# Attention over 16 heads: four engines' loops written out, SyncE's loads put behind its stores, DVE's scaling behind the last split

## What is computed

```python
h = _layernorm(x) * (1 + ca) + sa
Q = (h @ Wq + bq).reshape(B, S, Hn, Dh)         # B=1, S=4096, Hn=16, Dh=16; K and V alike
logits = jnp.einsum('bqhd,bkhd->bhqk', Q, K) * scale
logits = jnp.where(causal, logits, -jnp.inf)
attn = jax.nn.softmax(logits, axis=-1)
gate = jnp.tanh(g @ g_w2 + g_b2)[..., 0]
out = jnp.einsum('bhqk,bkhd->bqhd', attn * gate[:, None, None, :], V).reshape(B, S, E)
x = x + ga * (out @ Wo + bo)
```

## Time and profile before

| | us |
|---|---|
| median of 3 runs | 2980.59 |
| lowest and highest run | 2969.75, 2982.99 |
| profiled execution: span from first to last instruction | 2973.9 |
| PE busy | 2635.1 (89%) |
| DVE busy | 2263.6 (76%) |
| ACT busy | 1646.1 (55%) |
| POOL busy | 214.1 (7%) |

### The profile page before, as it was taken

How to read it: one execution, slowest core, us unless ns; L and a number is a source line. 1 busy time by engine, 2 the same in 40 slices (tenths; PEclk the granted TensorE clock), 3 DMA queues, 4 the chain that set the end, 5 groups by cost and what they waited for, 6 DMA issues and landing times. The chain is left out here.

```text
span 2973.9 us, 94419 instructions
## 1 busy us (share of the span) xinstructions
PE 2635.1 (89%) x36424; PEld 1624.7 (55%) x36424; DVE 2263.6 (76%) x4398; ACT 1646.1 (55%) x2421; POOL 214.1 (7%) x228
## 2 busy tenths in 40 slices
PE   6889999899989998999999978999997999218996
PEld 3332566666656665656557623555554666216774
DVE  3459898789979987999889933655555999685877
ACT  2320777677767776777677765111114777215663
POOL 1237000000000000000000020000000000000000
PEclk8985999999999999999999989999998999659998
DMA  4243011101110111011110001000000333413442
GB/s 141 95 96 72 3 27 28 25 7 28 27 28 4 27 27 28 10 21 27 28 28 5 6 4 53 29 14 28 14 0 8 96 99 103 124 29 100 119 122 64
DMA packets 158662, 133.50 MB, mean 45 GB/s; under 512 B 103097, under 2 KB 135996, under 8 KB 153276
## 3 DMA queue, kind: packets, MB, share of 16 engines
q1 hardware_dynamic: 152571, 124.08, 17.6%
q10 hardware_dynamic: 4224, 4.19, 0.4%
q0 software_dynamic: 1536, 0.40, 0.1%
HBM read 79.98 MB, written 46.66 MB: 43 GB/s over the span
## 5 line engine op out<-in xcount | busy, mean ns | idle before, releaser
L712 DVE TENSOR_REDUCE attn_pm<-attn_MS 128x1 f32<-128x512 f32 (+3 forms) x2304 | 1334.6, 640 | 171.0 <-PE attn_MS L756 144.2
L698 ACT ACTIVATE attn_PT<-attn_ES 128x1024 f32<-128x1024 f32 (+5 forms) x1152 | 1040.0, 951 | 370.8 <-PE attn_ES L791 366.5
L806 PE MATMUL attn_OP<-attn_PT,attn_VH 128*17 128x512 f32 (+3 forms) x4608 | 648.8, 562 | 0.2
L756 PE MATMUL attn_MS<-head_KX,head_QX 96*32 96x512 bf16 (+11 forms) x3456 | 399.4, 393 | 6.6 <-DVE attn_pm L712 3.5
L756 PE MATMUL attn_MS<-after_attention,attn_QX 96*32 96x512 bf16 (+10 forms) x2880 | 324.0, 358 | 2.8 <-issue 1.7
L791 PE MATMUL attn_ES<-head_QX,head_KX 99*32 99x512 bf16 (+8 forms) x3456 | 288.9, 368 | 41.7 <-issue 21.1
L756 PE MATMUL attn_MS<-attn_KX,attn_QX 96*32 96x512 bf16 (+7 forms) x2880 | 320.3, 371 | 1.3 <-DVE attn_pm L712 1.1
L791 PE MATMUL attn_ES<-attn_QX,after_attention 99*32 99x512 bf16 (+10 forms) x2880 | 244.0, 359 | 4.8 <-ACT attn_PT L698 4.4
L791 PE MATMUL attn_ES<-attn_QX,attn_KX 99*32 99x512 bf16 (+10 forms) x2880 | 242.2, 357 | 6.0 <-ACT attn_PT L698 4.4
L756 PEld LDWEIGHTS attn_MS<-head_KX,head_QX 96*32 96x32 bf16 x3456 | 158.8, 97 | 122.0 <-DVE attn_pm L712 59.1
L1195 PE MATMUL l0out_ring<-l0out_w,l0out_sT 128*128 128x512 f32 x512 | 225.0, 592 | 0.0
(11 more groups left out here) (295 smaller groups left out, 3363.8 us busy)
## 6 DMA issues: line engine op xcount, KB each, us to landing
vk_beta<-front_vk SPq DMA_DIRECT2D x8, 1024.0 KB, 4.1
kq_transposed<-l0out_w_in SPq DMA_DIRECT2D x8, 1024.0 KB, 5.0
delta_VK<-vk_beta SPq DMA_DIRECT2D x32, 256.0 KB, 2.8
delta_QK<-kq_transposed SPq DMA_DIRECT2D x32, 256.0 KB, 2.9
attn_QX<-qk_parts SPq DMA_DIRECT2D x60, 128.0 KB, 7.2
after_attention<-attn_out SPq DMA_DIRECT2D x18, 256.0 KB
x_res<-in_L_attn_x_dram ACTq DMA_DIRECT2D x8, 512.0 KB, 8.0
qk_parts<-project_hi SPq DMA_DIRECT2D x8, 512.0 KB, 2.9
```

The lines of the kernel that those rows point to most:

```text
L698: nc.scalar.activation(PT[u % NPT][:, 512 - wa:512 + wb], ES[half][:, 512 - wa:512 + wb], ACT.Exp, scale=DH ** -0.5).then_inc(exp_done, 1)
L712: nc.vector.tensor_reduce(pm[r][:, i, c:c + 1], MS[slot][:, 0:w], AX.X, ALU.max).then_inc(max_taken, 1)
L756: last = nc.tensor.matmul(MS[slot][r, 0:seen], QX[b][0:ROWS, i * P + 32 * g:i * P + 32 * g + 32], KX[b][0:ROWS, 512 * c:512 * c + seen], s ...
L806: last = nc.tensor.matmul(OP[32 * j:32 * j + DH + 1, 512 - w:512], VH[b][:, kt, :], PT[(2 * n + half) % NPT][:, o:o + w], start=(kt == 0), ...
```

## The change

It does three things, all in `attention`:

- PE, DVE, ACT and POOL run their 16 heads in Python loops, that is, written out. The hardware loops and the register arithmetic for wait values are gone from these four. SP keeps its loop.
- In SP's `turn`, the wait for `take_last` and the four stores of `last_rows` stand ahead of the wait for the head's last scores and the 12 loads of the head three later.
- DVE waits for the last head's split on POOL to be complete before `after_max`.

```diff
@@ sync, turn
-                if more:
-
-                    sp.wait_ge(exp_scores, HALVES * h + HALVES)
-                    sp.sem_inc(sheld, 1)
-                    load(h + NB, b)
                 sp.wait_ge(o_evac, 5 * h + 6)
                 sp.sem_inc(sheld, 1)
                 for j in range(TILES):
                     store(h, 1, j, j, last_out)
+                if more:
+                    sp.wait_ge(exp_scores, HALVES * h + HALVES)
+                    sp.sem_inc(sheld, 1)
+                    load(h + NB, b)
@@ gpsimd
-            with pool.Fori(0, H // NB) as i:
-                for b in range(NB):
-                    h = NB * i + b
-                    split_max(h, b, entry_count(h + 1, TURN_AT) + 1)
+            for h in range(H - 1):
+                split_max(h, h % NB, entry_count(h + 1, TURN_AT) + 1)
             split_max(H - 1, (H - 1) % NB, entry_count(H, 0) + 1)
@@ scalar
-            with act.Fori(0, H) as h:
+            for h in range(H):
                 for n in range(STEPS):
@@ vector
-            with dve.Fori(0, H // NB) as i:
-                for r in range(NB):
-                    stream(NB * i + r + 1, r)
+            for h in range(1, H):
+                stream(h, (h - 1) % NB)
             take_turned(H - 1, entry_count(H, 0), 0)
+            dve.wait_ge(split, 4 * H + 4)
             if after_max:
                 after_max(dve)
@@ tensor
-            with pe.Fori(0, TURNS) as i:
-                for b in range(NB):
-                    turn(NB * i + b, i, b, True, True)
-            for h in range(NB * TURNS, H):
-                turn(h, TURNS + (h - NB * TURNS) // NB, h % NB, h + 1 < H, h + 2 < H)
+            for h in range(H):
+                turn(h, h // NB, h % NB, h + 1 < H, h + 2 < H)
```

More of the change, by code:

```diff
@@ L605, in turn @@
                         first_loads(sp)
+                sp.wait_ge(o_evac, 5 * h + 6)
+                sp.sem_inc(sheld, 1)
+                for j in range(TILES):
+                    store(h, 1, j, j, last_out)
                 if more:
@@ L610, in turn @@
                     load(h + NB, b)
-                sp.wait_ge(o_evac, 5 * h + 6)
-                sp.sem_inc(sheld, 1)
-                for j in range(TILES):
-                    store(h, 1, j, j, last_out)
             for j in range(TILES):
```

## The result

The changed kernel takes **2902.55 us** (median of 4 runs, 2901.43 to 2903.43) where the kernel before takes 2978.89 on the same chip (4 runs, 2969.75 to 2982.99). The ratio is 0.9742, with a 95% interval of 0.9725 to 0.976. That is 76.3 us faster. The forecast was 64.8 us faster, at 2916.

The account below looks back on a forecast made before the run. PE was taken to set the pace, busy 90.7 of a clean head's 92.0 us. The terms 44.5 + 1.5 + 10 + 15.2 + 1.3 - 7.7 = 64.8 off 2980.6 gave 2916 us, range 2893 to 2940 (8 in 10).

Parts of the forecast that it names:

- Step 3: ACT's function table loaded once instead of 16 times, at the heads' starts: 10 us saved, ends 0 and 13.3.
- Steps 1 and 2: Branches back of PE and DVE gone in nine heads, 44.5 us saved; loop entry in head 0, 1.5 saved.
- Step 7: Register arithmetic for the loops gone from the heads: 0 us saved.
- Step 4: DVE's wait ahead of the last scaling: head 14 saves 12.7 us, head 15 saves 2.5, together 15.2.
- The rival that POOL's DMAs are held up: DVE's scaling blocks POOL's last DMA issue, so step 4 gives -0.5 instead of 15.2: 2932 us, chance 0.17.
- Steps 5 and 6: SP's stores ahead of loads, 1.3 us saved; late instruction fetches behind loads, 7.7 us lost, ends 0 and 20.
- The rival "all fetches in time": Straight code has all its instruction fetches in time, so step 6 is nothing: 2908 us, chance 0.13.
- Step 8: Blocks behind the attention, same code only placed elsewhere: cost 0, ends of 8 us either way.

Follow-up runs that it names:

- the loop over pairs: The changed kernel with ACT in a loop of 8 turns of two heads: 2919.16 us, ratio 0.9794, 16.6 slower than the change.

## Why the prediction was right, and where it was wrong

By the place where I put the savings, and by the head windows of the two kernels:

| place | predicted | measured |
|---|---|---|
| head 0 | 2.1 | 2.6 |
| the nine heads with a branch | 43.6 | 51.0 |
| heads 1 and 4 | -0.2 | 1.1 |
| heads 12 and 13 | 2.5 | 6.5 |
| head 14 | 13.3 | 14.0 |
| head 15 | 2.5 | 2.5 |
| blocks behind the attention | 0 | -5.0 |

(A predicted entry is made of the steps that fall in it: for the nine heads 44.5, and 9 times 0.6 less 0.7. Step 3's 10 is rounded, so they sum to 1.0 less than 64.8; 0.8 of the measured 73.5 lies at the attention's edges.)

*Steps 1 and 2, the branches* were right as a sum. No idle time of PE over 1.7 us is left in the attention (the longest is behind the last maximum, where PE waits for DVE), and the clock is 1.00. Of the nine heads' 51.0 us, 9 times 1.3 is what a clean head gained (step 3 below), and 5.2 of the 44.5 remain as small waits (821.5 for nine heads, 816.3 for nine clean ones).

*Step 3, the table load*, is the term that was mis-sized, and the largest miss: 10 predicted, and 1.3 in each of 15 heads measured (92.0 to 90.7), 19.5. The 1.3 has two parts. PE's wait of 0.8 behind ACT is gone, the 12 us that the step began with. And PE's busy time in a clean head fell from 90.7 to 90.2, for which I had nothing. I had taken 2 us off because PE would run into DVE, which worked 3.87 us without a gap. The rows refute that: PE's waits for DVE in a clean head are two of 0.2 before, with ACT alone written out, and after the change. What cut ACT's gain to between nothing and 0.6 in the old kernel were stops on "issue" of 0.4 to 0.8, one in each of heads 4, 7 and 10. Without them these heads would last 91.0 to 91.4. That these are late fetches, as those that went with the loads, is likely by their place and not shown. In the changed kernel the loop over pairs, with its load, cost 2.1 a turn, so there the table load can account for the whole 1.3. It is not shown to.

*Step 7, register arithmetic at nothing,* was right for each engine alone (91.9 and 92.1) and is open for the three together. The 0.5 us of PE's busy time that each clean head lost can be the registers', the table load's or both. There is no run with ACT and just one of the others written out, and POOL's loop was never written out alone.

*Step 4* was right in its mechanism and its sum: alone it was 15.2 and undone 14.0, and the rows of POOL, DVE and PE came as forecast. The split between its two terms was luck. With the wait alone head 14 gave 14.1 where I had 12.7, since without PE's wait of 13.81 it lasts 90.6 and not a clean head's 92.0. Head 15 gave nothing where I had 2.5 for the clock. In the whole change head 15 did become 2.5 shorter, but not surely by the wait: up to its last exponential it lasts 69.8 us in the change and 71.1 without the wait, but 71.0 and 70.9 in the kernels without loads and with the loop over pairs, which have it. The rival that POOL's DMAs are held up fell: their issue took 1.56 us while DVE multiplied. The Trainium skill, "SBUF — State Buffer", section "SBUF: two separate sides", says that DVE work with two SBUF inputs holds off only POOL work that reads SBUF, and the trace agrees: 14.73 us for the instruction that splits, 1.56 for the DMAs' issue. The case that it warns of, a DMA from POOL's queue held by DVE, did not occur here; by the rival it would have cost 16.

*Steps 5 and 6* were wrong in size and in their split. Together they were -6.4. I costed SP's shift at 1.3, its effect on one wait in one head, and wrote that moved loads "collide elsewhere but no less". Taken back, the shift is worth 11.2, and by the waits 2.8 of it are the rows' and 6.3 the stops' on "issue". What is left of late fetches is 2.3 us over 13 heads, 0.2 a head, where I had 0.7 and more. The excess of heads 1 to 13 over clean ones is 7.5, where the steps came to 11.1 (7.7, 0.3 for head 1 as it was, 1.3 and 1.8). The mechanism was right, in that without loads, or with spread ones, "issue" is gone. The rival "all fetches in time" (2908) came nearer than my sum, but not for its reason, since the fetches were late still. That the steps cost heads 1 to 13 too much shows in their length as well: I forecast 91.2 to 93, and they last 90.5 to 92.1. The Trainium skill's sentence that fetches in straight code are mostly hidden ("Runtime: NRT & Kernel Launch", section "Instruction fetch mechanics") agrees with 2.3 us in the 1435 of the attention, and less well with the 8.6 under SP's old order.

What I hadn't forecast is that the waits for POOL's rows are 4.7 us, in six heads. My step 5 spoke of one of 1.3. Without loads they are there just as much, so they don't come from the loads. That they come from a shorter path between the last maximum and the next head's first scores is argued. For it speaks that sending the parts one by one took them down to 1.0, and the transpose one piece earlier to 2.7.

*Step 8, the blocks behind*, cost 5.0 in the two profiles, 1153.9 to 1158.9, within my ends. The windows of that stretch, before, after, and in the kernel of before with only the wait:

```profile
1820.00:2973.90 1153.90, 940.84 (x8840) 612.76 (x8840) 806.17 (x1753) 476.69 (x1062) 29.42 (x39) 0.92 0.22 64
```
```profile
1741.50:2900.40 1158.90, 948.40 (x8840) 618.50 (x8840) 805.88 (x1753) 477.59 (x1062) 29.34 (x39) 0.91 0.22 63
```
```profile
1815.60:2976.90 1161.30, 948.79 (x8840) 619.54 (x8840) 805.93 (x1753) 476.37 (x1061) 29.34 (x39) 0.91 0.22 63
```

The third has the old code there but for a wait, and takes still longer, with the same share of work at the lower clock as the second. From the last exponential to the end, the profile of before has 1155.0 us, and the three with one engine's stream written out 1155.3, 1157.2 and 1157.6. The ten others, which have the new code or DVE's wait or both, have 1156.8 to 1162.4. So some 4 us may be a price of the change, and it is open of which part: the changed kernel without the wait has 1162.4 too.

In short, the errors are some 10 us too little for step 3 (with what of it is step 7's), 4 too much for late fetches and rows, and 5 for the blocks behind in the profiled pair: 64.8 + 10 + 4 - 5 is about the 73.5 of the spans.

The parts alone sum to 57.5. To that come 11.2 for SP's order. The 7.6 that are left are no more than the errors of these medians can make, as the interval of each ratio spans 3 to 7 us to either side, so the sum alone doesn't show that parts work only together. The rows do: with ACT alone a clean head gains 0 to 0.6 where the whole change gains 1.3, and with DVE alone PE stops for longer behind its branches (9.4 for 6.8).

## What to carry to other kernels

Cut the stage into its turns and find a clean one: the excess of the others over it priced the branches well (44.5). But price an item at the start of a turn in the kernel that is to be, where other engines' items there have gone too. A single edit on the old kernel can understate it: ACT's gave a clean head 0 to 0.6 us, where all together gave 1.3. And look at what takes a gain away: here it was not the engine that I had feared. When all engines are written out, put no block of loads where the instruction fetches and the next turn's small rows must pass, but spread it over the turn and send the rows as they come (9.1 us here for both).

## What the runs showed of the hardware that I had not expected

- A load of ACT's function table inside a loop is executed on every turn, even for the same function: 16 times, 8 with the loop over pairs, once when written out. Each turn of that loop, with its load, cost 2.1.
- Twelve loads in one block fill the DMA engines to 0.90 for some 12 us (the window below, of head 1 in the changed kernel), and the instruction fetches among them come up to 12.7 us apart instead of about 7. PE stands on "issue" for 0.3 to 1.1 us at four places in this kernel, and for up to 2.3 with SP's old order.

```profile
397.90:410.00 12.10, 12.10 (x220) 6.12 (x212) 11.19 (x20) 9.38 (x10) 0.00 (x0) 1.00 0.90 138
```

- A POOL instruction of 0.52 us was held for 14.73 us by six separate DVE instructions, the longest of 8.67, as though no gap between them let it in, and this came out the same in two kernels. A DMA issue of POOL was not held at all.
